# A graph network's last stage: deeper rings for the attention sums, fewer semaphores for the row gathers, and score scatters behind the first gathers

## The reference, cut to what matters

```python
Wh = einsum('ni,hio->hno', h, W)                 # per node and head
e_l, e_r = Wh @ a_l, Wh @ a_r                    # two scores per node and head
e = leaky_relu(e_l[:, src] + e_r[:, dst]) + log(clip(edge_weight, 1e-8))
alpha = exp(e - segment_max(e, dst)[dst])
alpha = alpha / (segment_sum(alpha, dst)[dst] + 1e-8)
out = segment_sum(alpha * Wh[src], dst) + bias   # 6250 x 128
x = x + out
```

## Time and profile before

| | us |
|---|---|
| median of 3 runs | 8103.16 (8084.32 to 8224.06) |
| the profiled execution | 8091.68 |
| its span | 8089.9 |

### The profile page before, as it was taken

How to read it: one execution, slowest core, us unless ns; L and a number is a source line. 1 busy time by engine, 2 the same in 40 slices (tenths; PEclk the granted TensorE clock), 3 DMA queues, 4 the chain that set the end, 5 groups by cost and what they waited for, 6 DMA issues and landing times.

```text
span 8089.9 us, 151519 instructions
## 1 busy us (share of the span) xinstructions
PE 5318.0 (66%) x44994; PEld 4663.3 (58%) x44994; DVE 3863.3 (48%) x6044; ACT 2333.4 (29%) x6489; POOL 1739.8 (22%) x1693
## 2 busy tenths in 40 slices
PE   2888888888888999999999996000114531533255
PEld 2666666666667999999999995000013421432245
DVE  7999999988884222111111113000214731833478
ACT  3887777777773111110000002000000000000005
POOL 1000000000000000000000002766777266165330
PEclk9999999999999999999999996555556865866688
DMA  4345555566666666666676662333445554555465
GB/s 133 128 177 197 207 220 229 233 237 234 238 242 277 261 261 267 277 275 276 275 277 277 278 278 54 102 96 102 125 126 174 142 157 120 135 168 137 120 181 157
DMA packets 509526, 1587.66 MB, mean 196 GB/s; under 512 B 167402, under 2 KB 195148, under 8 KB 482319
## 3 DMA queue, kind: packets, MB, share of 16 engines
q1 hardware_dynamic: 425422, 1351.59, 45.5%
q0 software_dynamic: 55376, 121.59, 6.3%
q10 hardware_dynamic: 28298, 109.21, 3.6%
HBM read 972.87 MB, written 609.23 MB: 196 GB/s over the span
## 4 chain that ended last, share of the span: by engine, by line
PE 54%; issue 20%; another core or an unknown queue 9%; DVE 8%; ACT 4%; ACTq 2%; DVEq 1%; DMA 1%; SPq 0%; POOL 0%; POOLq 0%
PE psum L1079 27%; PE psum L1045 10%; PE psum L1049 9%; ACT arena L861 3%; PE psum L1207 3%; DVE arena L1830 2%; DVE arena L1840 1%; PE psum L1039 1%; ACTq L861 1%; ACTq L837 1%; DVE arena L1827 1%; DVE quad_place L1823 1%; DVEq L1840 0%; PE psum L1145 0%
## 5 line engine op out<-in xcount | busy, mean ns | idle before, releaser
L1079 PE MATMUL psum<-arena,H 128*128 128x128 f32 x19208 | 2252.8, 277 | 14.6 <-issue 14.6
L1079 PEld LDWEIGHTS psum<-arena,H 128*128 128x128 f32 x19208 | 2230.1, 188 | 14.8 <-issue 14.8
L861 ACT COPY arena<-psum x4704 | 1857.6, 410 | 504.3 <-PE psum L1049 383.8
L735 POOL DMA_INDIRECT H<-head_table,H x1568 | 1575.6, 1005 | 1138.4 <-issue 537.2
L1207 PE MATMUL psum<-arena 128*128 128x132 f32 x5088 | 871.2, 325 | 1287.3 <-issue 525.7
L1207 PEld LDWEIGHTS psum<-arena 128*128 128x128 f32 x5088 | 745.0, 223 | 1412.9 <-issue 807.4
L1039 PE MATMUL psum<-zero_b 128*128 128x2 bf16 x4704 | 789.1, 168 | 375.5 <-ACT arena L861 364.5
L1049 PE MATMUL psum<-arena 128*128 128x200 bf16 x4704 | 815.9, 255 | 0.0
L1039 PEld LDWEIGHTS psum<-zero_b 128*128 128x128 bf16 x4704 | 457.0, 97 | 614.6 <-issue 526.7
L1049 PE MATMUL psum<-H,arena 128*128 128x200 bf16 x4704 | 807.7, 253 | 0.0
L1476 DVE TENSOR_TENSOR H<-H,work 128x9408 bf16<-128x9408 bf16 x147 | 742.6, 5052 | 0.0
(11 more groups left out here) (291 smaller groups left out, 4089.4 us busy)
## 6 DMA issues: line engine op xcount, KB each, us to landing
arena<-adj SPq DMA_DIRECT2D x196, 3200.0 KB, 10.0
adj<-arena SPq DMA_DIRECT2D x1176, 400.0 KB
arena<-edge_rows SPq DMA_DIRECT2D x636, 272.0 KB
edge_rows<-H ACTq DMA_DIRECT2D x196, 544.0 KB
H<-head_table,H POOLq DMA_INDIRECT x1568
arena<-in_edge_attr SPq DMA_DIRECT2D x4, 3072.0 KB, 15.6
quad_rec<-edge_records SPq DMA_DIRECT2D x636, 10.0 KB
head_table<-arena SPq DMA_DIRECT2D x7, 476.0 KB
```

The costliest lines, as they stand in the source:

```text
L735: pool.indirect_dma_start(out=rows[:, j, :], out_offset=None, in_=head_table, in_offset=bass.IndirectOffsetOnAxis(ap=idx_stage[:, j:j + 1] ...
L861: act.copy(evac[:, :, bass.ds(place, SEG)], banks[:, bass.ds(bank, NSEG * SEG)].rearrange("p (w c) -> p w c", w=NSEG)).then_inc(pair_copie ...
L1079: mm = pe.matmul(ps_y[slot][:, 0:D], source[:, hi, :], adj_in[slot][:, :, 2 * hi:2 * hi + 2], start=(hi == 0), stop=(hi == NB - 1))
```

## The change

1. Quad steps: 12 row slots instead of 6, 6 one-hot buffers, places and PSUM banks instead of 3 (4), and DVE prepares 5 steps ahead of the sum instead of 2. The loop body stays at 12 steps. The buffers move: the one-hots into `work`, some softmax vectors into weights that are no longer needed.
2. `row_landed` becomes 2 semaphores, one for each half, instead of 16. ACT has one wait for a half instead of eight.
3. POOL's order at the start of the stage: 35 scatters, then the first iteration of row gathers, then the other 14 scatters and the 5 gathers of `right0`.

```diff
-QRING = 6
-QBODY = 2 * QRING
+QRING = 12
+QBODY = QRING
+QBANKS = 6
+AHEAD = QBANKS - 1
...
-        row_landed = [sem(f"row_landed{j}") for j in range(RING)]
+        row_landed = [sem(f"row_landed{i}") for i in range(2)]
...
-            for b in range(BLOCKS):
-                ... scatter b ...
-            pool.wait_ge(dst0_ready, 1)
-            pool.wait_ge(right_stored, 16)
-            for c in range(NC): ... gather right0[c] ...
+            def scatter_right(first, end): ... the same loop ...
+            scatter_right(0, BLOCKS - 2 * GROUP)
             pool.wait_ge(heads_stored, 16 * GROUPS)
...
-                        .then_inc(row_landed[j], 16)
+                        .then_inc(row_landed[j // HALF], 16)
             run_gathers(0)
+            scatter_right(BLOCKS - 2 * GROUP, BLOCKS)
+            pool.wait_ge(dst0_ready, 1)
+            pool.wait_ge(right_stored, 16)
+            for c in range(NC): ... gather right0[c] ...
...
-                        for j in range(half * HALF, (half + 1) * HALF):
-                            act.wait_ge(row_landed[j], k * 16 + (16 * (ITER0[c] + 1)))
+                        act.wait_ge(row_landed[half], k * (16 * HALF) + (16 * HALF * (ITER0[c] + 1)))
...
-                            mm = pe.matmul(ps[j % 3][:, 0:AGG_W], quad_onehot[:, j % 3, q, :],
+                            mm = pe.matmul(quad_ps[j % QBANKS], quad_onehot[:, j % QBANKS, q, :],
...
-                    dve.wait_ge(quad_partial, n + (QRING - 3))
+                    dve.wait_ge(quad_partial, n + (QRING - QBANKS))
...
-                        if j + 2 < QBODY or ahead:
-                            prepare(k, j + 2)
+                        if j + AHEAD < QBODY or ahead:
+                            prepare(k, j + AHEAD)
                         add(k, j, at)
-                prepare(0, 0)
-                prepare(0, 1)
+                for j in range(AHEAD):
+                    prepare(0, j)
```

More of the change, by code:

```diff
@@ L79 @@
 QUADS = [P * n // QUAD for n in SPAN]
-QRING = 6
-QBODY = 2 * QRING
+QRING = 12
+QBODY = QRING
+QBANKS = 6
+AHEAD = QBANKS - 1
+assert QBODY % QBANKS == 0
 QITERS = [-(-(n + BLOCKS - 1) // QBODY) for n in QUADS]
@@ L205, in build @@
         quad_rec = sb("quad_rec", [P, QRING, 4 * REC])
-        quad_place = sb("quad_place", [P, 4, 4])
+        quad_place = sb("quad_place", [P, QBANKS, 4])
         Hflat = H[:, :, :].rearrange("p b f -> p (b f)")
@@ L265, in build @@
         record = [piece(SM * REC) for _ in range(2)]
-        same_b, keep_b = piece(SM + 1), piece(SM + 1)
-        piece = carve(arena[:, 0:BLOCKS * D])
+        same_b, keep_b, dst_b = piece(SM + 1), piece(SM + 1), piece(SM + 2)
+        piece = carve(arena[:, 0:BLOCKS * ROW3])
         quad_rows = piece(QRING * 4 * ROW3).rearrange("p (s q f) -> p s q f", s=QRING, q=4)
-        quad_onehot = piece(3 * 4 * P).rearrange("p (s q d) -> p s q d", s=3, q=4)
-        fwd_b, bwd_b, dst_b = piece(SM), piece(SM), piece(SM + 2)
+        quad_onehot = work[:, :, :].rearrange("p i f -> p (i f)")[:, 0:QBANKS * QUAD].rearrange("p (s q d) -> p s q d", s=QBANKS, q=4)
+        piece = carve(w_all[:, NC - 1:, :].rearrange("p k f -> p (k f)"))
+        fwd_b, bwd_b = piece(SM), piece(SM)
         psum = ctx.enter_context(nc.psum_tensor("psum", [P, 8 * BANK], F32))
@@ L274, in build @@
         banks = psum[:, 0:BANKS * BANK]
+        quad_ps = [psum[:, i * BANK:i * BANK + AGG_W] for i in range(QBANKS)]
         ps_tab = psum[:, BANKS * BANK:(BANKS + 1) * BANK]
@@ L709, in _, with scatter_right @@
             pool.wait_ge(starts_ready, 1)
-            for b in range(BLOCKS):
[L711 to L715, removed]
-            pool.wait_ge(dst0_ready, 1)
-            pool.wait_ge(right_stored, 16)
[L719 to L722, removed]
+            def scatter_right(first, end):
+                for b in range(first, end):
+                    if b % GROUP == 0:
+                        pool.wait_ge(heads_ready, b // GROUP + 1)
+                    pool.indirect_dma_start(out=right_edges, out_offset=bass.IndirectOffsetOnAxis(ap=first_edge[:, b:b + 1], axis=0),
+                                            in_=right[:, b, :], in_offset=None, bounds_check=E_PAD - 1, oob_is_err=False)\
+                        .then_inc(right_scattered, 16)
+            scatter_right(0, BLOCKS - 2 * GROUP)
             pool.wait_ge(heads_stored, 16 * GROUPS)
@@ L736, in run_gathers @@
                                             in_offset=bass.IndirectOffsetOnAxis(ap=idx_stage[:, j:j + 1], axis=0))\
-                        .then_inc(row_landed[j], 16)
+                        .then_inc(row_landed[j // HALF], 16)
             run_gathers(0)
+            scatter_right(BLOCKS - 2 * GROUP, BLOCKS)
+            pool.wait_ge(dst0_ready, 1)
+            pool.wait_ge(right_stored, 16)
+            for c in range(NC):
+                pool.indirect_dma_start(out=right0[:, c, :], out_offset=None, in_=right_table,
+                                        in_offset=bass.IndirectOffsetOnAxis(ap=dst0[:, c:c + 1], axis=0),
+                                        bounds_check=BLOCKS * P - 1, oob_is_err=False).then_inc(right0_loaded, 16)
             with pool.Fori(1, SPAN_ITERS) as k:
@@ L969, in _ @@
                     rec = quad_rec[:, slot, :].rearrange("p (q r) -> p q r", r=REC)
-                    act.wait_ge(quad_landed[slot], k * 64 + (32 * (QSTEP0[NC - 1] // QRING + j // QRING + 1)))
-                    act.wait_ge(quad_ready, n - 4)
-                    act.activation(quad_place[:, j % 4, :], rec[:, :, HEADS3], ACT.Identity,
+                    act.wait_ge(quad_landed[slot], k * 32 + (32 * (QSTEP0[NC - 1] // QRING + j // QRING + 1)))
+                    act.wait_ge(quad_ready, n - QBANKS)
+                    act.activation(quad_place[:, j % QBANKS, :], rec[:, :, HEADS3], ACT.Identity,
                                    bias=quad_off[:, NC - 1, bass.ds(k * QBODY + j, 1)]).then_inc(quad_placed, 1)
@@ L1721, in _ @@
             dve.wait_ge(quad_row_loaded, 32)
-            dve.sem_inc(quad_added, 3)
+            dve.sem_inc(quad_added, QBANKS)
             def softmax(i):
@@ L1817, in prepare @@
                     rec = quad_rec[:, slot, :].rearrange("p (q r) -> p q r", r=REC)
-                    place = quad_place[:, j % 4, :]
-                    dve.wait_ge(quad_landed[slot], k * 64 + (32 * (QSTEP0[i] // QRING + j // QRING + 1)))
+                    place = quad_place[:, j % QBANKS, :]
+                    dve.wait_ge(quad_landed[slot], k * 32 + (32 * (QSTEP0[i] // QRING + j // QRING + 1)))
                     last_chunk = i == NC - 1
@@ L1828, in prepare @@
                     dve.wait_ge(quad_placed, n)
-                    dve.wait_ge(quad_partial, n + (QRING - 3))
-                    dve.tensor_tensor(quad_onehot[:, j % 3, :, :],
+                    dve.wait_ge(quad_partial, n + (QRING - QBANKS))
+                    dve.tensor_tensor(quad_onehot[:, j % QBANKS, :, :],
                                       iota[:, :].rearrange("p (a d) -> p a d", a=1).to_broadcast([P, 4, P]),
@@ L1837, in add @@
                     dve.wait_ge(quad_partial, n + (1 + QRING))
-                    dve.wait_ge(quad_added, n + 3)
+                    dve.wait_ge(quad_added, n + QBANKS)
                     a = AGG[:, bass.ds(at[j], 1), :].rearrange("p a f -> p (a f)")
-                    dve.tensor_tensor(a, a, ps[j % 3][:, 0:AGG_W], ALU.add)\
+                    dve.tensor_tensor(a, a, quad_ps[j % QBANKS], ALU.add)\
                         .then_inc(quad_added, 1)
@@ L1856, in quad_sums @@
                 body(QITERS[i] - 1, False)
-                dve.wait_ge(quad_added, QSTEP0[i + 1] + 3)
+                dve.wait_ge(quad_added, QSTEP0[i + 1] + QBANKS)
             for i in range(NC):
```

## The result

The changed kernel took 8307.58 us (median of 4, 8296.49 to 8318.24), the kernel before beside it 8126.75 (8084.32 to 8224.06): 1.0212 times as long, with a 95% interval of 1.0131 to 1.0294. That is slower beyond the noise; whether by more than 2% this pair alone does not say. The profiled execution took 8309.84, its span is 8308.0 against 8089.9.

What follows compares the result with a forecast made beforehand. The sums, slowed beside gathers by the crawl, were taken to set each phase's end. Terms: +4 (POOL's order), -62 (ACT's waits), +98 (longer crawl) = +40, so 8132 us profiled, 8140 forecast for the median; range 7885 to 8350.

Steps and rivals of the forecast that it cites:

- rival (3): Path behind the gathers: without ACT's stalls POOL itself is held to 1.4 us a gather; +242, about 8345 us; chance 0.17.
- phase 1: First phase of gathers beside the previous chunk's sums: the crawl lasts through its gathers, 696 against 647 us, +49.
- POOL's order: Start of the stage: the second iteration of row gathers starts at 5087.5 instead of 5083.2; +4 us, between 0 and +8.
- ACT's waits: Chunk 0: with 13 queue instructions instead of 21, ACT no longer makes POOL wait; -62 us, at worst 0.
- the crawl: Slow mode beside gathers: PE, ACT and SP take 1.4 us an instruction; without POOL's stalls it lasts through them, +98 us.
- the step which I had called the first that could fail: From "ACT's stalls came before each end of a crawl" to "they ended it"; the +98 us of the four phases follow.
- the gathers' pace: POOL's row gathers: 1.257 us each when not stalled, giving chunk 0 603 instead of 667 us and 1.26 in the phases.
- The rings: Deeper quad-step buffers: 3 more steps beside each phase's gathers, nothing in the four tails and chunk 4.
- Rival (1): Phases: POOL stalls for something else, so modes keep alternating; -70, up to -140 us, about 8030; chance 0.26.
- Rival (2): Phases: the crawl goes away, steps take 2.15 us beside gathers of 1.48; -529 us, about 7575; chance 0.13.
- Rival (4): Whole stage: the crawl comes of the recording, so the change does nothing beyond +4 us; about 8107; chance 0.07.

Runs made afterwards that it cites:

- the repeated run: Changed kernel once more on a crawling chip, with lower bounds on two waits: 8293.16 us, 1.0368 times the kernel before; its profiled execution took 8105.32.
- the spacing: Kernel before with a 240-element POOL memset behind each row gather: 7621.10 against 7995.93 us (0.9527) on a crawling chip, 1.0290 on a calm one.

## Why the prediction came out as it did

The direction was right, and so was the mechanism in its main step; the size was not: +40 us was forecast, +218 came, in the profiled executions. The measured 8308 lies within the range of 7885 to 8350, but that is little merit: the range was wide enough to hold rival (3)'s 8345, and slower by more than 2% had been given only 0.17. By stages, forecast and measured:

| | forecast | measured |
|---|---|---|
| start and chunk 0, to the first quad matmul | -58 | -23 |
| phase 1, to its last add | +49 | +115 |
| phase 2 | +14 | +45 |
| phase 3 | +24 | +52 |
| phase 4 | +11 | +29 |
| chunk 4 | 0 | 0 |

**POOL's order** (+4) held: the second iteration of gathers starts 45.7 us behind the staged indices, against 40.8 before. That is +4.9. The stage as a whole began 5.4 us earlier in the execution after, which no term of the sum had; it is in the table's first row.

**ACT's waits** held as a mechanism: ACT's stalls vanished, and with them the ends of the crawl. In chunk 0 of the kernel before, ACT's slow instructions end at 5175, 5309, 5467, 5578 and 5691, and the last stall of each group of POOL's ends at 5175, 5309, 5466, 5578 and 5690. The run that gave ACT its instructions back (and used eight semaphores) on a crawling chip was level with the kernel before, and its traced execution has ACT's stalls and the taking of turns again. That supports the step which I had called the first that could fail. It does not isolate it: that run changed two things, and it ran on another chip than the changed kernel. On a calm chip the semaphores alone are worth only some 28 us, against the 258 between 8293.16 and 8035.18, but what they are worth on a crawling one was not measured. Nor does every phase crawl to its end without these stalls: the brisk phase of the repeated run had none.

**What was mis-sized** is the gathers' pace. I took 1.257 us for every gather not stalled. The runs showed that a crawling chip serves one gather in about 1.40 us. POOL can run ahead of that for a while, and then it is held itself. That cost 41 us in chunk 0 (464 gathers in 624 us, not 583) and 52 in chunk 1 (516 us, not 464); the gathers of the later phases, each behind a rest, lost 15, 12 and 5 (377, 314 and 186 us against 362, 302 and 181). Second, I let the crawl end with the last gather. It went on for 17 to 27 us behind it, four times; in the kernel before it had been 4 to 8. These terms come to more than the 178 us that were missing, in part because the tails behind them were 4 to 12 us shorter than forecast. Rival (3) had the debt and the 1.40 us in chunk 0, and its 8345 is nearer to the 8308 measured than my 8140. It was a little too dear because I made every phase pay 0.14 us more for each gather; rests of 225 to 298 us in front of chunks 2 to 4 pay the debt back.

**The rings** gave no more than the three steps a phase of the forecast: PE's timeline shows single instructions at 1.4 us, so depth hides nothing. They were not run alone on a crawling chip. At the start of a phase five steps are prepared ahead, each behind loads that take SP some 10 us in the crawl. The first matmul is no later for it: it starts 76 us behind chunk 0's last gather in both kernels. The first add is: it comes 50 us behind that matmul instead of 8, where I had 4.6 us for the longer lead.

**Rival (1)** fell: no other stall of POOL took the place of ACT's; those of 2 us, once in 112 gathers, did not end the crawl. **Rival (2)** fell for the changed kernel on a crawling chip, one phase of the repeated run apart, but it is what a calm chip does all the time, and what the spacing brings about: steps below 2 us beside the gathers, and POOL as the bound. **Rival (4)** fell on its number, that nothing would change, but not on its premise, that the crawl comes of the recording. I had held 8103 against 8090 against it. Every execution here has a span and a clock of its own from the recording, so both are times of recorded executions, and their agreement says nothing of an unrecorded one. What the runs do show is that the program alone does not decide: the same one crawls on some chips and not on three others, on which it is 8 per cent faster.

So the explanation now is: on a crawling chip the path behind POOL's gathers serves one in 1.40 us. POOL alone asks for one in 1.26, and the difference piles up. While it does, a queue gets one instruction through in 1.4 us when it asks for more. Stalls of POOL drain it: ACT's in the kernel before, the rests at the ends of phases, or a spacing that never lets it fill. The change took away the first of these. The two paces and the effect of the spacing are measured; that something piles up is argued, since no trace shows it. The queues do not all slow together. Beside the first phase's gathers (5850 to 6200) ACT asks for one queue instruction in 1.75 us in the changed kernel and is never slowed, while in chunk 0 of the kernel before it asked for one in 1.07 and was. Nor does the crawl wait until POOL is held: ACT's first slow instruction there comes 43 us behind the first gather, and in the changed kernel POOL keeps its pace for some 250 us.

Open: what the path is, and why one chip has the 1.40 us and another not. The Trainium skill, "NOTIFIC — the notification-queue block", section 7.1, would let a full record path hold its producers back; every execution here was recorded, so none shows whether that is what these runs met.

## What to carry to other kernels

A stall can be what keeps another resource alive. Before you remove one, ask what drains during it, and look at the rates: a producer that runs 10 per cent faster than the path behind it is served may need a brake rather than a faster partner. Compare a kernel on more than one chip before you tune it for a mode that it shows on one: here the same program differed by 8 per cent between chips, and each chip has another best version.

## What the hardware showed that I had not expected

- A chip-dependent mode in which the busy queues get one instruction through in 1.4 us while gathers run, and in the changed kernel for 17 to 27 us after them (a matmul with its weight load every 2.8 us). A queue that asks for fewer is spared: ACT's with 13 instructions for an iteration had none that was slow, with 21 a third of them. On three chips no trace has this mode.
- In it a memset of 0.32 us with its semaphore wait behind each gather, pure waste by its own account, makes the kernel before 4.7 per cent faster.
- Row gathers that count on only two semaphores stall 2.1 to 3.5 us once in every 112 gathers. With eight semaphores the longest wait is 1.3 us, with sixteen 0.3. With sixteen and the spacing's three instructions such stalls of some 2 us come back, one in every 98 gathers. What counts up to these numbers I don't know.
- A gather's time on POOL rises from 0.95 to 1.25 us beside VectorE's one-hot comparison, and not beside its multiplication, though both read two inputs in SBUF. Where in the gather the overlap falls was not varied, and beside no one-hots there were only 23 such gathers.
